# Reordering the set-up of a transformer block kernel: where the first statistics, the weight transposes and batch 1's transposes stand

## What is computed

```python
mod = (_silu(L0_c) @ L0_wmod).reshape(L0_c.shape[0], 6, 1, -1)
sa, ca, ga, sb, cb, gb = (mod[:, 0], ...)
h = _layernorm(x, axis=-1) * (1 + ca) + sa
x = x + ga * _L0_attn_ref(h, Wq, bq, Wk, bk, Wv, bv, Wo, bo)
h = _layernorm(x, axis=-1) * (1 + cb) + sb
x = x + gb * _L0_ffn_ref(h, weight, bias)
```

## Time and profile before

| | |
|---|---|
| median of 3 runs | 305.88 us (305.63 to 306.06) |
| profiled execution: its own time | 306.11 us |
| profiled execution: span from first to last instruction | 304.4 us |
| busy share of the span: TensorE, VectorE, ScalarE, GpSimd | 85%, 88%, 68%, 71% |
| mean granted clock of TensorE | 0.948 of full speed |

### The profile page before, as it was taken

How to read it: one execution, slowest core, us unless ns; L and a number is a source line. 1 busy time by engine, 2 the same in 40 slices (tenths; PEclk the granted TensorE clock), 3 DMA queues, 4 the chain that set the end, 5 groups by cost and what they waited for, 6 DMA issues and landing times.

```text
span 304.4 us, 4341 instructions
## 1 busy us (share of the span) xinstructions
PE 259.2 (85%) x1324; PEld 161.5 (53%) x1324; DVE 268.7 (88%) x348; ACT 206.9 (68%) x551; POOL 216.5 (71%) x154
## 2 busy tenths in 40 slices
PE   3898995998969868989998999899979758998394
PEld 1654453366536613664566457645755346875273
DVE  3879699969998999899999999999999989989821
ACT  1586775877797976987998799766747264637310
POOL 6101529984989989799989998999998999514200
PEclk9999996999999997999999999999979966999879
DMA  7633975794964389236962694369437942302024
GB/s 239 170 149 100 358 203 178 245 349 123 338 165 129 103 251 300 91 103 200 330 200 83 217 329 134 79 227 322 134 106 215 302 138 72 98 6 86 1 71 138
DMA packets 54387, 53.90 MB, mean 177 GB/s; under 512 B 4094, under 2 KB 52812, under 8 KB 54364
## 3 DMA queue, kind: packets, MB, share of 16 engines
q1 hardware_dynamic: 54364, 53.63, 56.6%
HBM read 44.89 MB, written 8.72 MB: 176 GB/s over the span
## 4 chain that ended last, share of the span: by engine, by line
DVE 47%; PE 22%; issue 11%; POOL 9%; ACT 7%; DMA 2%; SPq 0%; DVEq 0%; POOLq 0%; ACTq 0%
DVE prod L1402 18%; DVE pv_buf L1517 12%; POOL pv_buf L588 5%; PE ps L885 5%; DVE prod L1391 3%; PE ps L849 3%; PE ps L710 2%; PE ps L787 2%; ACT x_norm L988 2%; DVE ps L1410 2%; DMA pv_buf<-in_L_wmod 2%; DVE ps L1489 1%; DVE ps L1493 1%; DVE ps L1488 1%; PE ps L817 1%
## 5 line engine op out<-in xcount | busy, mean ns | idle before, releaser
L588 POOL TENSOR_TENSOR pv_buf<-pv_buf 128x1024 f32<-128x1024 f32 (+2 forms) x63 | 137.8, 2187 | 21.0 <-DVE pv_buf L1517 16.7
L1402 DVE TENSOR_TENSOR prod<-ps,kT 128x1024 f32<-128x1024 f32 (+4 forms) x70 | 75.4, 1112 | 0.0
L1517 DVE TENSOR_TENSOR pv_buf<-v_shift,ps 128x1024 f32<-128x1024 f32 x49 | 59.5, 1214 | 0.0
L805 PE MATMUL ps<-prod,sel_sum 128*32 128x512 f32 x256 | 31.9, 621 | 7.0 <-DVE prod L1402 7.0
L849 PE MATMUL ps<-wo_g,w_raw 128*128 128x256 f32 x128 | 33.4, 406 | 0.0
L710 PE MATMUL ps<-hT,wT 128*128 128x512 f32 x64 | 30.7, 622 | 0.9 <-ACT hT L1078 0.8
L737 PE MATMUL ps<-wT,h_cen 128*128 128x256 f32 x128 | 29.6, 379 | 0.0
L721 PE MATMUL ps<-hT,wT 128*128 128x512 f32 x64 | 29.4, 600 | 0.0
L849 PEld LDWEIGHTS ps<-wo_g,w_raw 128*128 128x128 f32 x128 | 24.1, 198 | 6.7 <-issue 3.9
L737 PEld LDWEIGHTS ps<-wT,h_cen 128*128 128x128 f32 x128 | 24.0, 190 | 6.5 <-issue 3.8
L885 PE MATMUL ps<-wf_g,w_raw 128*128 128x256 f32 x80 | 20.5, 400 | 0.0
(11 more groups left out here) (180 smaller groups left out, 552.9 us busy)
## 6 DMA issues: line engine op xcount, KB each, us to landing
v_shift<-v_rows SPq DMA_DIRECT2D x56, 512.0 KB, 5.4
x_in<-in_L_attn_x SPq DMA_DIRECT2D x8, 512.0 KB, 3.9
v_rows<-v_base SPq DMA_DIRECT2D x8, 512.0 KB, 4.3
x_res<-in_L_attn_x SPq DMA_DIRECT2D x8, 512.0 KB, 6.4
out_x<-outb SPq DMA_DIRECT2D x5, 512.0 KB, 5.2
rows_mod<-mod_rows SPq DMA_DIRECT2D x7, 256.0 KB, 3.2
x<-in_L_wmod SPq DMA_DIRECT2D x1, 1024.0 KB, 6.3
row_ga<-mod_rows SPq DMA_DIRECT2D x8, 128.0 KB, 4.4
```

Source lines behind the costliest of these rows:

```text
L588: nc.gpsimd.tensor_tensor(dst, dst, ring(b, n)[:, t:NT, :], ALU.add).then_inc(s_add, 1)
L805: mm = nc.tensor.matmul(ps23[32 * g:32 * g + 32, 1, :], sel_sum[:, which, c, :], prod[:, n, c, :], start=(c == 0 and which == 0), stop=(c ...
L1402: nc.vector.tensor_tensor(prod[:, n, :, o:L], ps01[:, :, o:L], kT[:, b % 2, :, 0:L - o], ALU.mult).then_inc(s_prod, 1)
L1517: nc.vector.tensor_tensor(dst[:, t:NT, :].rearrange("p t (h e) -> p t h e", e=DH), v_n.rearrange("p t (h e) -> p t h e", e=DH), weights, A ...
```

## The change

No instruction is added or removed; the lists of TensorE, ScalarE and VectorE are put in another order. VectorE: the statistics of batch 0's x come before silu, and Wk's copy before the copy of the modulation columns. TensorE: Wk's transposes come before the modulation product, Wq's behind batch 0's transposes of h, Wv's behind the first half of q; batch 1's transposes of h come behind all three sets of batch 0's head sums. ScalarE follows: Wv's copy behind the first half of k, and batch 1's `h_modulated` behind `copy_scores(0)`. SP's and POOL's lists are unchanged.

```diff
--- before.py
+++ after.py
@@ -260,7 +260,7 @@
         CONST_SUM = CONST_EARLY + 4 * NC
         CONST_ALL = CONST_SUM + NO + 1
         SETUP_SILU, SETUP_COLS, SETUP_WF, SETUP_MOD, SETUP_ROWS = 3, 5, 11, 12, 16
-        PE_COND, PE_MOD, PE_WK, PE_COLS, PE_WQ, PE_WV, PE_ROWS, PE_WO, PE_WF = range(1, 10)
+        PE_COND, PE_WK, PE_MOD, PE_COLS, PE_WQ, PE_WV, PE_ROWS, PE_WO, PE_WF = range(1, 10)
         NGATED = 5
         NLN1, NRS1, NLN2, NLN2D, NRS2 = 3, 2, 2, 3, 2
         NPOST = 3
@@ -662,17 +662,15 @@
                                                  ident[:, :])
                 mm.then_inc(s_pset, 1)
 
+            weight_transposes(1)
             pe.wait_ge(s_cset, SETUP_SILU)
             pe.wait_ge(s_wmod[0], 16)
             modulation(ps45, wmod_cols, P)
-            weight_transposes(1)
             pe.wait_ge(s_cset, SETUP_COLS - 1)
             nc.tensor.transpose(ps23[:, 1, 0:P], mod_cols, ident[:, :])
             pe.wait_ge(s_small, 48)
             mm = nc.tensor.transpose(ps23[:, 1, P:P + 3 * NC], bias_rows[:, :], ident[0:3 * NC, 0:3 * NC])
             mm.then_inc(s_pset, 1)
-            weight_transposes(0)
-            weight_transposes(2)
 
             def first_h_transposes():
                 pe.wait_ge(s_cset, SETUP_COLS)
@@ -905,9 +903,12 @@
                 ffn_products(LAST, half_, ps01, True)
 
             first_h_transposes()
-            for j in (1, 0):
-                k_rows(0, j)
-                q_rows(0, j)
+            weight_transposes(0)
+            k_rows(0, 1)
+            q_rows(0, 1)
+            weight_transposes(2)
+            k_rows(0, 0)
+            q_rows(0, 0)
             v_rows(0, 1)
             v_rows(0, 0)
             pe.wait_ge(s_wmod[1], 16)
@@ -915,10 +916,10 @@
             modulation(ps67, wmod_rows, D)
             weight_transposes(3)
             head_sums(0, 0)
+            head_sums(0, 1)
+            head_sums(0, 2)
             h_transposes(1, 1)
             h_transposes(1, 0)
-            head_sums(0, 1)
-            head_sums(0, 2)
             scores_by_token(0)
             k_rows(1, 1)
             k_rows(1, 0)
@@ -1191,8 +1192,8 @@
             first_norm()
             h_modulated(0, 1)
             h_modulated(0, 0)
+            evacuate_k(0, 1)
             evacuate_weight(2)
-            evacuate_k(0, 1)
             centre_h(0)
             sums_before(1)
             evacuate_k(0, 0)
@@ -1201,9 +1202,9 @@
             evacuate_v(0, 0)
             evacuate_weight(3)
             norm_before(1)
+            copy_scores(0)
             h_modulated(1, 1)
             h_modulated(1, 0)
-            copy_scores(0)
             seed_q(1)
             centre_h(1)
 
@@ -1313,6 +1314,9 @@
                 nc.vector.tensor_tensor(dst, dst, diff, ALU.add).then_inc(done, 1)
                 assert k[0] == NLN2D
 
+            dve.wait_ge(s_xin, 16)
+            variance(x_in, negmean1, var1, s_ln1d, s_var1)
+
             link, k = chain(s_cset, 0, 0)
 
             dve.wait_ge(s_aset, 1)
@@ -1323,15 +1327,13 @@
                                          silu_r[:, :].rearrange("p (k b) -> p k b", b=B), ALU.mult))
             assert k[0] == SETUP_SILU
 
-            dve.wait_ge(s_xin, 16)
-            variance(x_in, negmean1, var1, s_ln1d, s_var1)
-
-            dve.wait_ge(s_pset, PE_MOD)
-            link(nc.vector.tensor_copy(mod_cols, ps45[:, 0, 0:P]))
-
             def evacuate_qk_weight(i):
                 dve.wait_ge(s_pset, PE_WK if i == 1 else PE_WQ)
                 nc.vector.tensor_copy(wT[:, i, :, :], turned_weight(i)).then_inc(s_wqk, 1)
+
+            evacuate_qk_weight(1)
+            dve.wait_ge(s_pset, PE_MOD)
+            link(nc.vector.tensor_copy(mod_cols, ps45[:, 0, 0:P]))
 
             dve.wait_ge(s_pset, PE_COLS)
             nc.vector.tensor_copy(bias_cols[:, :], ps23[:, 1, P:P + 3 * NC])
@@ -1339,7 +1341,6 @@
             nc.vector.tensor_copy(cols8[:, :, 0:NC], by_cols[:, 0:B, 0:NC])
             link(nc.vector.tensor_scalar(cols8[:, :, NC:2 * NC], by_cols[:, 0:B, NC:2 * NC], 1.0, None, ALU.add))
             assert k[0] == SETUP_COLS
-            evacuate_qk_weight(1)
             dve.wait_ge(s_qopen, 1)
             for j in (1, 0):
                 nc.vector.tensor_copy(ps01[:, j, :],
```

## The result

| | before | after |
|---|---|---|
| median | 306.37 us, 7 runs (305.63 to 306.76) | 308.39 us, 7 runs (307.22 to 309.81) |
| ratio, 95% interval | | 1.0068 [1.0043, 1.0093] |
| profiled execution, its span | 306.11, 304.4 us | 308.39, 306.7 us |
| mean granted clock | 0.948 | 0.95 |

What follows compares the result with a forecast made beforehand. VectorE was taken as the bound, with 47% of the chain. Products 0, exponentials 0.05 and batch 1's softmax 1.1 on 306.11 gave 307.2; less 0.23 for the median, 307.0 us, range 305.4 to 308.8.

Steps and rivals of the forecast that it cites:

- Slower, through batch 3's x: SP's queue: v's 1.6 delay reaches batch 3's x, less 0.43 swallowed; batch 1's softmax +1.1; likeliest case, chance 0.48.
- Products 0 to +0.1: Set-up, first q*k products on VectorE: start at 17.6 as before, 0 to +0.1, their 2.27 of idle time used up.
- The 1.8 won by the early statistics: Set-up on VectorE: statistics begun at 4.3 give normalised x some 1.8 earlier, all lost waiting for the columns.
- Batch 0's exponentials 0 to +0.1: Batch 0's softmax: head sums win 0.4, lost to ScalarE's list; exponentials at about 36.8 instead of 36.71.
- The delay is kept from there: After batch 1's softmax: the chain lies mostly on VectorE, so the +1.1 stays to the end.
- The late rise: TensorE's full clock comes during k: products at 19.1, v 3.1 late, batch 1's softmax +2.6, total 308.5; chance 0.17.
- Faster, through a missed fall of the clock: Near the end, 287.9 to 293.0: TensorE's work misses the half clock, 2.5 less, total 304.5; chance 0.13.

Runs made afterwards that it cites:

- k_first: The changed kernel with ScalarE's second copy of batch 0's k ahead of batch 1's sums instead of behind them; 308.02 us, ratio 1.0065.
- only_sums: The kernel before with only batch 0's head sums together and ScalarE's `copy_scores(0)` ahead of batch 1's `h_modulated`; 305.77 us, ratio 0.9990.
- x3_early: The changed kernel with the load of batch 3's x issued ahead of SP's wait for the biases' round trip; 307.85 us, ratio 1.0057.
- wv_only: The kernel before with Wv's transposes behind the first half of q and its ScalarE copy behind the first copy of k; 309.80 us, ratio 1.0102.
- sums_x3: The kernel before with the head sums together and batch 3's x loaded ahead of the wait for the biases' round trip; 305.25 us, ratio 0.9971.
- fill: The changed kernel with fourteen extra identity transposes on TensorE, results unread: eleven ahead of Wk, one behind the product, two behind the columns; 307.71 us, ratio 1.0037.

## Why the prediction was right, and where it was too low

**Slower, through batch 3's x: right, and shown.** Predicted were v 1.6 late, the whole queue with it, less 0.43 swallowed by ScalarE's wait for k. The measured chain is 2.36 (v), 2.22 (load), 2.30 (sums), 1.73 (softmax): each step passes on what it gets, and the swallowing is there (two waits of 1.74 and 0.43 became one of 3.15). k_first shows it from the side of v (v +1.28, sums +1.24, softmax +0.69), only_sums from the side of the pin. x3_early shows that the load sets the sums; its softmax hangs on VectorE. Taken behind the first products, v is late by 4.75 - 3.17 = 1.58, against 1.6. These are marks of single traces; no pair of medians tells the load's part from zero.

**Products 0 to +0.1: mis-sized, +0.78.** The step counted on Wk's landing 4.2 after its issue. In this execution it took 4.9, and in my own account the landing stood on the path: Wk, product, columns (11.57 + 0.17 = 11.74 against 11.0), x's transposes (11.79 against 11.05), Wq. Before, half of such a 0.7 would have met a TensorE busy with the product (until 7.74, and 3.2 + 4.9 is 8.1); the change puts all of it at the head. Over all the traces here the same load took between 4.1 and 4.9. I had read one landing as if it were a constant, and gave the term no upper bound. The 1.8 won by the early statistics is lost to the wait for the columns, as said, and VectorE's own 3.7 behind Wq's copy follows as said (14.65 + 3.73 = 18.38).

**Batch 0's exponentials 0 to +0.1: +0.92**, of which 0.78 came with the products; the softmax itself is only 0.50 late, so what the sums won (0.3) is lost to ScalarE, as the step had it. only_sums is fairer to this step: there the exponentials are 1.09 sooner; that this is because Wv's copy doesn't push ScalarE is argued, not tested.

**The delay is kept from there: nearly.** 1.73 becomes 1.63 up to batch 6, then 1.83 at batch 7, and the last 0.44 comes behind that, among the stretches at half clock. They stand a little elsewhere in every trace, so this may belong to the execution as much as to the change; that wasn't separated.

**The late rise: given 0.17, and there in all, though it need not cost.** With the set-up's order as it was, the rise came at 10.84 to 13.40 in four traces of four, always ahead of k, which took 1.96. With any of its moves, and nothing filled in, it came at 14.43 to 19.49 in nine of nine, the changed kernel's 14.63 among them, and k took 2.41 to 3.75 in the other eight. So the moves in the set-up go with a later rise, by an amount that differs between executions. What that costs one of them ranges from nothing (the changed kernel's trace) to 1.8 on k and 1.0 on q (wv_only). How often it costs the changed kernel something wasn't measured, and its median doesn't ask for it: the profiled execution, at 308.39 on the median, lost nothing on k. Nor does its spread prove much: of the executions of before beside the experiments, the slowest took 308.27.
The term itself was priced from a wrong reading. Four of k's did not take 3.14 in the earlier trace rows: that is the part of them which lies in the window from 51.2 to 54.4, and the fourth ended behind it. At the lower level throughout, four take 3.75, which is 1.8 more than in the earlier trace rows, not 1.2.
I expected gaps in TensorE's work to decide the rise. wv_only has nearly no gap ahead of x's transposes, only four transposes fewer than before, and it rose 5.6 after k began, later behind k than any other. What decides it is open.
The Trainium skill (TensorE: Matmul & The Clock Gate, "Part 4: PE-mode transpose") says that full clock does not engage for transposes. In sums_x3 TensorE had done nothing but transposes from 8.2, and the clock rose at 10.84 in the middle of them; in the trace of before it rose at 13.40 behind 3.7 of them. That speaks against it as a flat rule. Whether these transposes run in the mode that the page means, no trace here shows.

**Faster, through a missed fall of the clock: no.** The stretch near 288 did meet less work, 3.40 us against 5.38, by an estimate 1 us less of loss, and the one at 225 was missed in full. But the one near 250 met 8.97 against 5.47. In sum TensorE did 12.4 us of late work at the lower level against 14.3 before, and the end is still later: the amount alone doesn't decide. The rival looked at one fall of the clock where there are three.

## What to carry over

Before moving work ahead of something late, find what paces the next few batches; here it was one load deep in SP's list, behind two round trips. The kernel with the head sums together and that load moved up came out faster than before (0.9971); none of those with a move in the set-up and without the early load did. And ask what stands right beside the pin: here, 0.4 us away, TensorE's k at half clock. A wait put at the head of an engine's list makes the landing of its load part of the path, and then the spread of that landing belongs in the range. If a part of a change delays ScalarE by one copy, follow the list to the last instruction behind it: Wv's copy cost v 1.6 us although TensorE had the weight in time.

## What the runs showed of the hardware

The same 256 KB load, issued at the same time behind the same loads, landed 4.1 to 4.9 us later, from one execution to another. TensorE's rise after the start is not fixed by the program: with the same lists up to k (the changed kernel, k_first, x3_early) it came at 14.63, 15.42 and 17.18 in three executions, and k took 1.97, 2.69 and 3.21. The clock column read 1.00 throughout, because the trace has no clock record ahead of the rise; the start of the first record and the durations show it. Transposes follow the clock too: eight of x's took 1.91 at the lower level (before) and 1.31 at the upper (sums_x3).

Near 115 us the clock was granted at 0.75 in the trace of before and 0.50 in that of fill over the same 6.8 us, and fill's delay grew by 0.9 across it, as much as many an edit at the start. One kernel alone varies so as well: of the 29 executions of before beside sums_x3, the two at a mean granted clock of 0.961 took 304.83 and 305.09, those at 0.948 to 0.950 took 305.94 to 307.08.
